# Three of a tile's eight row one-hots made on ScalarE, in the PEER stage of a two-layer decoder

## The reference, cut to what matters

```python
q = (x @ Wq + bq).reshape(B, S, N_HEADS, D_QUERY)      # 8 heads, two halves of 32
s1 = jnp.einsum('bshd,nd->bshn', q1, K1)               # 64 keys each
s2 = jnp.einsum('bshd,nd->bshn', q2, K2)
v1, i1 = jax.lax.top_k(s1, TOPK)                       # TOPK = 10
v2, i2 = jax.lax.top_k(s2, TOPK)
all_scores = (v1[..., :, None] + v2[..., None, :]).reshape(...)
all_indices = (i1[..., :, None] * N_SQRT + i2[..., None, :]).reshape(...)
vals, best = jax.lax.top_k(all_scores, TOPK)
expert_idx = jnp.take_along_axis(all_indices, best, axis=-1)
scores = jax.nn.softmax(vals, axis=-1)
h = jnp.einsum('bsd,bshkd->bshk', x, W_down[expert_idx])
h = jax.nn.gelu(h, approximate=False) * scores
out = jnp.einsum('bshk,bshkd->bsd', h, W_up[expert_idx])
```

## Time and profile before

| | us |
|---|---|
| median of 3 runs | 3727.76 (3727.37 to 3727.78) |
| the profiled execution | 3728.29 |
| its span (first to last instruction) | 3726.5 |
| PEER stage's regular part: one tile's period, from one last `weigh` to the next (1586.19 to 1633.61) | 47.42 |
| VectorE busy in 1400 to 1800 of the span | 389.70 of 400 |
| TensorE busy there | 369.43 of 400 |
| POOL and ScalarE busy there | 304.67 and 108.68 of 400 |

### The profile page before, as it was taken

One profiled execution on the slowest core, in us unless ns is written; L12 is line 12 of the kernel. 1 busy time (PEld: TensorE's weight loads), 2 busy tenths in 40 slices (PEclk: granted clock), 3 DMA queues, 4 the chain that ended last, 5 costly groups with the idle time before them and its releaser, 6 DMA issues. The chain is left out here.

```text
span 3726.5 us, 93465 instructions
## 1 busy us (share of the span) xinstructions
PE 3259.4 (87%) x33694; PEld 2767.7 (74%) x33695; DVE 2724.6 (73%) x10791; ACT 1198.5 (32%) x3136; POOL 2145.3 (58%) x2454
## 2 busy tenths in 40 slices
PE   6999968776499999999999999878888799799998
PEld 4777745554488888888888888865555587799998
DVE  6666634454999999999999999948888577433333
ACT  1434435543222222222222222215565322122221
POOL 4444435551577777777777777767887233233333
PEclk8999979997799999999999999989999799899999
DMA  5444424443000000000000000015554131566665
GB/s 153 110 122 125 106 70 118 123 114 125 1 2 2 2 2 2 2 2 2 2 2 2 2 2 2 2 37 134 133 129 118 55 117 53 144 181 182 183 184 131
DMA packets 255729, 277.62 MB, mean 74 GB/s; under 512 B 43870, under 2 KB 200286, under 8 KB 254814
## 3 DMA queue, kind: packets, MB, share of 16 engines
q1 hardware_dynamic: 241694, 253.40, 23.5%
q0 software_dynamic: 13632, 18.91, 3.5%
HBM read 187.34 MB, written 72.29 MB: 70 GB/s over the span
## 5 line engine op out<-in xcount | busy, mean ns | idle before, releaser
L1262 POOL TENSOR_TENSOR peer_hot_v<-peer_hot_e,peer_parts 80x512 bf16<-80x512 bf16 x768 | 991.0, 1316 | 323.8 <-DVE peer_hot_e L1305 314.4
L1081 PE MATMUL peer_ps_u<-peer_up,peer_g 128*128 128x256 f32 x2048 | 533.7, 407 | 0.6 <-DVE x_all L1403 0.6
L1062 PEld LDWEIGHTS peer_ps_h<-peer_xnT,peer_down 128*128 128x128 f32 x4096 | 509.3, 196 | 15.6 <-DMA peer_down<-in_peer_down 1.0
L1062 PE MATMUL peer_ps_h<-peer_xnT,peer_down 128*128 128x128 f32 x4096 | 509.1, 279 | 0.7 <-DMA peer_down<-in_peer_down 0.7
L1072 PE MATMUL peer_ps_w<-peer_hot_v,peer_hot_u 80*128 80x32 bf16 x12288 | 347.5, 177 | 151.6 <-DVE peer_g L1317 103.2
L1072 PEld LDWEIGHTS peer_ps_w<-peer_hot_v,peer_hot_u 80*128 80x128 bf16 x12288 | 337.2, 97 | 173.4 <-issue 92.8
L1081 PEld LDWEIGHTS peer_ps_u<-peer_up,peer_g 128*128 128x128 f32 x2048 | 393.1, 202 | 53.3 <-issue 1.0
L1159 ACT ACTIVATE peer_g<-peer_ps_h 128x512 f32<-128x512 f32 x256 | 152.8, 597 | 842.5 <-PE peer_ps_h L1062 842.1
L1309 DVE TENSOR_TENSOR peer_hot_u<-peer_count,peer_uvT 80x2048 bf16<-80x2048 bf16 x256 | 348.7, 1362 | 0.0
L2237 POOL DMA_INDIRECT out<-moe_y,moe_target x71 | 112.5, 1585 | 312.5 <-DVE moe_y L2336 309.7
L2181 PE MATMUL moe_ps_t<-moe_xgT,moe_w 128*128 128x128 f32 x2272 | 266.7, 276 | 0.0
(11 more groups left out here) (370 smaller groups left out, 7084.2 us busy)
## 6 DMA issues: line engine op xcount, KB each, us to landing
moe_w<-in_moe_w SPq DMA_DIRECT2D x142, 512.0 KB, 4.5
causal_qs<-causal_qscratch SPq DMA_DIRECT2D x32, 384.0 KB, 3.9
cross_qs<-cross_qscratch SPq DMA_DIRECT2D x32, 384.0 KB, 3.6
band_qs<-band_qscratch SPq DMA_DIRECT2D x32, 384.0 KB, 3.9
route_w<-in_moe_w SPq DMA_DIRECT2D x8, 1024.0 KB, 5.9
causal_qscratch<-causal_part SPq DMA_DIRECT2D x32, 192.0 KB, 2.7
causal_kscratch<-causal_part SPq DMA_DIRECT2D x32, 192.0 KB, 2.0
causal_ks<-causal_kscratch SPq DMA_DIRECT2D x32, 192.0 KB, 4.2
```

The source lines that it names most:

```text
L1062: mm = nc.tensor.matmul(ps_h[:, n % 2, k * P:(k + 1) * P], down[:, c, 4 * n + k, :], xnT[:, par, c, :], start=(c == 0), stop=(c == DC - 1))
L1081: mm = nc.tensor.matmul(ps_u[:], g[:, par, v, :], up[:, v, :], start=(v == 0), stop=(v == EV - 1))
L1262: ins = nc.gpsimd.tensor_tensor(hot_v[0:SEL, n % RING, part], hot_e[0:SEL, n % RING], w, ALU.mult)
```

## The change

`ON_ACT = (0, 2, 6)` names the pieces whose `hot_u` ScalarE now makes. For each of the piece's 16 tokens there is one ACTIVATE with the function Square, input `count` and a per-partition bias of -u: it writes (count - u) squared, 80 x 128 in bf16, into every second element of the piece's `hot_u`. One ACTIVATE with the function Relu over the whole piece in place, 80 x 2048, with scale -1 and bias 1, makes 1 of every 0, and 0 of every other square. Between them ScalarE waits for its own 16th Square. `take_uvw` gains one ACTIVATE that writes -u (`minus_u`). VectorE leaves `hots` after `hot_e` for these pieces; TensorE waits for the one or the other semaphore; the scratch `rest` of POOL is reused in place, which makes room for `minus_u`.

```diff
+ON_ACT = (0, 2, 6)
+def made(t, n, on_act):
+    mine = [k for k in range(NCH) if (k in ON_ACT) == on_act]
+    return len(mine) * t + sum(k <= n for k in mine)
...
             def weights(t, n):
-                pe.wait_ge(u_ready, NCH * t + n + 1)
+                pe.wait_ge(u_act_ready if n in ON_ACT else u_ready, made(t, n, n in ON_ACT))
...
             def take_uvw(t, par):
                 act.wait_ge(uvw_done, t + 1)
-                wait(act, u_ready, NCH * (t - 1))
+                wait(act, u_ready, made(t - 2, NCH - 1, False))
+                wait(act, u_act_ready, made(t - 2, NCH - 1, True))
...
+                nc.scalar.activation(minus_u[0:SEL, :], ps_q[0:SEL, 0:P], ACT.Copy, scale=-1.0)
...
+            def hots(t, n):
+                act.wait_ge(uvw_used, t + 1)
+                wait(act, w_done, NCH * t + n + 1 - RING)
+                for k in range(CHUNK):
+                    token = n * CHUNK + k
+                    ins = nc.scalar.activation(hot_u[0:SEL, n % RING, k // 2, :, k % 2], count[0:SEL, :, 0], ACT.Square,
+                                               bias=minus_u[0:SEL, token:token + 1])
+                ins.then_inc(squared, 1)
+                act.wait_ge(squared, made(t, n, True))
+                flat = hot_u[0:SEL, n % RING].rearrange("p a b c -> p (a b c)")
+                nc.scalar.activation(flat, flat, ACT.Relu, bias=iota[0:SEL, 1:2], scale=-1.0).then_inc(u_act_ready, 1)
...
             def macro(t, par):
                 for n in range(NCH):
+                    if n + AHEAD in ON_ACT:
+                        hots(t, n + AHEAD)
+                    if n + AHEAD - NCH in ON_ACT and there(t + 1):
+                        hots(t + 1, n + AHEAD - NCH)
...
# VectorE, hots
                                         vt, ALU.is_equal).then_inc(e_ready, 1)
+                if n in ON_ACT:
+                    return
                 wait(dve, w_done, NCH * t + n + 1 - RING)
```

More of the change, by code:

```diff
@@ L953, in peer_stage @@
         wT = sb("wT", [P, P])
-        rest = sb("rest", [P, 2, P])
+        rest = sb("rest", [P, P])
         parts = sb("parts", [P, 2, 3, P], BF16)
@@ L961, in peer_stage @@
         mark = sb("mark", [P, 1])
+        minus_u = sb("minus_u", [P, P])
         ps_q = ps("ps_q", [P, 512])
@@ L989, in peer_stage @@
         u_ready = sem("u_ready")
+        u_act_ready = sem("u_act_ready")
+        squared = sem("squared")
         e_ready = sem("e_ready")
@@ L1175, in take_uvw @@
                 act.wait_ge(uvw_done, t + 1)
-                wait(act, u_ready, NCH * (t - 1))
+                wait(act, u_ready, made(t - 2, NCH - 1, False))
+                wait(act, u_act_ready, made(t - 2, NCH - 1, True))
                 wait(act, v_ready, NCH * (t - 1) + 1)
                 nc.scalar.activation(uvT[0:SEL, par, :, :].rearrange("p k s -> p (k s)"), ps_q[0:SEL, 0:2 * P], ACT.Copy)
+                nc.scalar.activation(minus_u[0:SEL, :], ps_q[0:SEL, 0:P], ACT.Copy, scale=-1.0)
                 nc.scalar.activation(parts[0:SEL, par, 0, :], ps_q[0:SEL, 2 * P:3 * P], ACT.Copy)
                 nc.scalar.activation(wT[0:SEL, :], ps_q[0:SEL, 2 * P:3 * P], ACT.Copy).then_inc(uvw_used, 1)
+            def hots(t, n):
[9 more added lines that the diff above has]
+                nc.scalar.activation(flat, flat, ACT.Relu, bias=iota[0:SEL, 1:2], scale=-1.0).then_inc(u_act_ready, 1)
             def first():
+                act.wait_ge(roots_ready, 1)
                 for t in range(2):
@@ L1193, in first @@
                 take_uvw(0, 0)
+                for n in range(AHEAD):
+                    if n in ON_ACT:
+                        hots(0, n)
             def macro(t, par):
                 for n in range(NCH):
+                    if n + AHEAD in ON_ACT:
+                        hots(t, n + AHEAD)
+                    if n + AHEAD - NCH in ON_ACT and there(t + 1):
+                        hots(t + 1, n + AHEAD - NCH)
                     if there(t + 2):
@@ L1225, in split @@
                 pool.wait_ge(uvw_used, t + 1)
[L1226 to L1229, removed]
+                steps.link(nc.gpsimd.tensor_tensor(rest[0:SEL, :], wT[0:SEL, :], parts[0:SEL, par, 0, :], ALU.subtract))
+                steps.link(nc.gpsimd.tensor_copy(parts[0:SEL, par, 1, :], rest[0:SEL, :]))
+                steps.link(nc.gpsimd.tensor_tensor(rest[0:SEL, :], rest[0:SEL, :], parts[0:SEL, par, 1, :], ALU.subtract))
+                steps.link(nc.gpsimd.tensor_copy(parts[0:SEL, par, 2, :], rest[0:SEL, :]))
             def norm(t):
```

## The result

| | before | after |
|---|---|---|
| median | 3727.57 us (4 runs) | 3634.28 us (4 runs, 3633.05 to 3639.95) |
| ratio, 95% interval | | 0.9751, 0.9739 to 0.9763 |
| span of the profiled execution | 3726.5 | 3632.6 |
| a tile's mean period (from one L1438 add, L1403 before, to the next) | 47.47 | 44.37 |
| ScalarE busy in 1200 to 2200 of the span | 265.25 | 729.36 |

The account below looks back on a forecast made before the run. VectorE was taken as the bound at 47.42 us a tile, TensorE at 43.8; less 3.54 for three compares, plus 0.5 for waits, gives 44.4. Over 31 tiles 93 us go, so 3634 us; range 3604 to 3690.

Parts of the forecast that it names:

- The bound: PEER stage: VectorE binds the 47.42 us period, falling to 43.9 without three compares; TensorE stands behind at 43.8.
- The Square: One 128-column ACTIVATE on ScalarE: a pitch of 0.28 to 0.29 us, with ends of 0.16 and 0.40.
- The Relu and the piece: On ScalarE: 1.98 us for 2048 columns; with 16 Squares and a 0.2 wait, 6.7 us in all.
- ScalarE's loop: ScalarE's three pieces in one round with TensorE: 22.8 + 3P, 42.9 us a tile, one microsecond under VectorE's 43.9.
- P: ScalarE's time for one piece of `hot_u`, forecast at 6.7 us; its round with TensorE becomes the bound at 7.0.
- The point of balance: ScalarE's piece time at which the gain is gone and the period is the old 47.42: 8.2 us.
- Rival 2: ScalarE's Squares don't overlap: 0.40 us each, a piece 8.6, 3766 us, slower; decides from 0.375; chance 0.08.
- The meeting points: VectorE's `halves` needs `take_s`, met by a few tenths; `hot_e` of piece 0 needs `take_uvw`, met or 0.1 late.
- A sign that I had named against me: TensorE's `weights` of pieces 0, 2 or 6 held by ScalarE's `hot_u` would show the forecast wrong.
- The added 0.5: Microseconds a tile added because VectorE and TensorE wait for each other and `take_s` and `take_uvw` have no slack: 44.4.
- POOL and the compares: Change in blocking between POOL and VectorE as compares start earlier: counted as zero, with 0.7 us either way.
- Tiles: 31 of 32 counted as regular in the PEER stage, 3.0 us saved in each: 93 us.

Follow-up runs that it names:

- floor: Changed kernel without ScalarE's one-hots, and TensorE turns x ahead of `weights` of piece 1: 3639.94 us, 0.9757 of the kernel before.
- only pieces 0 and 6: Changed kernel with ScalarE making `hot_u` of pieces 0 and 6, VectorE keeping piece 2: 3659.56 us, 0.9801 of the kernel before.

## Why the prediction was right, point by point

- **The bound.** VectorE, with TensorE close behind: right. With two compares gone the period fell by what they took (2.30 less, 2.28 measured); with all three by 3.10, and TensorE's own busy time went to 97% of it. Its floor of 43.8 held a slow stretch in itself, as the forecast says: it is busy for 42.45 in the 44.07 tile, at full clock, and for 43.46 in the 44.72 one.
- **The Square.** 0.285 forecast, 0.292 measured. `take_q`, the row of the same form, was the right one to go by: 0.258 and 0.03 for SBUF. The ends, 0.16 and 0.40, would have given 4.7 and 8.6 a piece.
- **The Relu and the piece.** 1.98 and 2.00; 6.7 and 6.85. The Trainium skill, ScalarE: Activation LUTs, section Rules for kernel authors, budgets about 0.3 us and 0.83 ns an element for an ACTIVATE, an estimate of 0.41 for a Square. That is near the duration of one, 0.426, but not the pitch in a run, so the 8.5 that it gives for a piece did not come. The same page, section What ACT_TABLE_LOAD costs, gives 280 ns and 0.833 ns an element, and an overlap of 93 ns back to back: an estimate of 294 ns, and the pitch is 292.
- **ScalarE's loop.** The mechanism and its place were right, its price too low by 1.1 to 1.5 us at P of 7.6 and 8.0, as I read it for want of the slow clock behind some of the waits. The point of balance is near 7.8, not 8.2. At 6.85 it didn't matter. Rival 2 was nearer than I had put it: the Square would have had to be 0.35, not 0.375.
- **The meeting points.** Forecast as met by a few tenths or 0.1 late. In 1200 to 2200 of the changed kernel `take_s` is late 3 times, by up to 0.23, and `take_uvw` 8 times by 0.16, in some 22 tiles.
- **A sign that I had named against me showed, without harm.** I had written that I am wrong if `weights` of pieces 0, 2 or 6 are held by ScalarE. They are, before pieces 2 and 6, for 0.6 us a tile, and the kernel without ScalarE's one-hots is no faster. I had not traced the way from piece 6 to its own `weights`.
- **The added 0.5.** The term had about the right size (3.54 less 0.44), and that was partly luck. It was a guess, given to two engines that wait for each other and to meeting points without slack. The waits at the meeting points are real, but only 0.14 of it. The other 0.3 are terms that the forecast had elsewhere or not at all: compares of 3.43 rather than 3.54, `hot_e` longer by 0.17, the product `uvw` by 0.03.
- **POOL and the compares.** Counted as zero, which was near: a compare of 2.06 beside POOL's work is still there, at piece 4 for piece 3, and one of 1.37 at piece 3 for the 1.34 of piece 2. What changed is 0.1 less on the compares (1.26 forecast for piece 2, 1.16 in the run with it alone) and 0.17 on `hot_e`. The Trainium skill, SBUF — State Buffer, section Who interferes with whom, calls the pair of ports that VectorE shares with POOL an exclusive lock held for a whole instruction. The two lengths, 1.21 and 2.06, agree with it; no run here tries it.
- **Tiles.** 31 by 3.0 is 93; it was 28 by 3.09 and 7.4 at the ends, 93.9. That the total came to the microsecond is luck: the period was forecast to 0.1, which is 3 us.

## What to carry to other kernels

Room on an engine is not its idle share. Follow the new work once round the loop in which it stands (here TensorE, gelu, three pieces, TensorE) and compare that sum, with its multiple of the new work's price, with the bound: some 12 us of idle time a tile held 0.9 us a piece. And check an offload by its two halves, the removal alone and the added work made longer: the first says what it costs now, the second how far it is from turning over.

## What the runs showed of the hardware

- An ACTIVATE with a bias from memory that reads and writes every second bf16 element, 128 of them, has a pitch of 0.292 us in a run of 16 (`take_q`, the nearest row, had 0.258 from PSUM); with 2048 columns in place it takes 2.00.
- A wait of 2.02 us on TensorE was followed by a stretch at half clock that took 1.7 us more. Shortening a wait from 0.97 to 0.70 didn't keep the clock up in one kernel (floor), and in the changed kernel `output` takes 1.89 behind one wait of 0.97 and 2.93 behind one of 0.96: the length of the last wait alone doesn't decide.
- With VectorE free of waits (only pieces 0 and 6) the period is 45.19 in tiles with TensorE at a mean clock of 1.00 and of 0.96.
